# A bidirectional recurrence: the order in which TensorE and ScalarE take its keys, values and gate inputs

## The reference, cut to what matters

```
def step(carry, kv):                      # a, b, m start at 0, 0, -1e38
    mm = maximum(m + w, kt)
    e1 = exp(m + w - mm)
    e2 = exp(kt - mm)
    return ((e1 * a + e2 * vt, e1 * b + e2, mm), (a, b, m))
...
kk = kt + u
M = maximum(maximum(mf, mb), kk)
ef, eb, ec = exp(mf - M), exp(mb - M), exp(kk - M)
y = (ef * af + eb * ab + ec * vt) / (ef * bf + eb * bb + ec)
```

## Time and profile before

| | |
|---|---|
| time, median of 3 runs | 491.46 us (491.12 to 492.39) |
| profiled execution, its own time | 496.69 us |
| its span, first to last instruction | 494.8 us |
| mean granted TensorE clock | 0.81 |
| TensorE busy | 400.9 us (81%) |
| VectorE busy | 391.2 us (79%) |
| ScalarE busy | 228.1 us (46%) |
| GpSimd busy | 121.9 us (25%) |

### The profile page before, as it was taken

How to read it: one execution, slowest core, us unless ns; L and a number is a source line. 1 busy time by engine, 2 the same in 40 slices (tenths; PEclk the granted TensorE clock), 3 DMA queues, 4 the chain that set the end, 5 groups by cost and what they waited for, 6 DMA issues and landing times.

```text
span 494.8 us, 9007 instructions
## 1 busy us (share of the span) xinstructions
PE 400.9 (81%) x3570; PEld 283.6 (57%) x3570; DVE 391.2 (79%) x883; ACT 228.1 (46%) x391; POOL 121.9 (25%) x182
## 2 busy tenths in 40 slices
PE   4677857989777989999992998696799178798976
PEld 4676727769663667766761443234368036656965
DVE  3899999589887845498787679988899859777974
ACT  4477373644836668845511296010293022362261
POOL 3525344042242225233313026602202020000000
PEclk9968885596757989999986899896699578588686
DMA  8545000004014000200000000000000000000000
GB/s 279 222 121 231 2 2 1 1 1 146 1 29 191 2 1 1 95 2 1 1 0 2 1 0 0 0 1 1 1 1 1 1 1 1 1 1 2 11 24 33
DMA packets 4237, 17.53 MB, mean 35 GB/s; under 512 B 858, under 2 KB 1763, under 8 KB 3683
## 3 DMA queue, kind: packets, MB, share of 16 engines
q1 hardware_dynamic: 4194, 16.95, 9.4%
HBM read 16.16 MB, written 0.79 MB: 34 GB/s over the span
## 4 chain that ended last, share of the span: by engine, by line
PE 42%; DVE 38%; ACT 8%; issue 6%; POOL 4%; DMA 1%; SPq 0%; DVEq 0%; ACTq 0%; POOLq 0%
PE PS L1523 36%; DVE R L1102 4%; POOL rstd L522 3%; PE PS L1655 2%; DVE R L1374 2%; DVE R L1376 2%; DVE R L995 2%; PE PS L1662 2%; DVE R L1427 1%; DMA T<-tok_w 1%; DVE Q L1092 1%; DVE stats L1005 1%; DVE stats L958 1%; POOL ve L519 1%; DVE xn L1015 1%
## 5 line engine op out<-in xcount | busy, mean ns | idle before, releaser
L1523 PE MATMUL PS<-Q,R 128*128 128x32 f16 (+3 forms) x1024 | 46.1, 191 | 13.7 <-DVE R L1102 10.2
L1523 PE MATMUL PS<-m,Q 128*128 128x192 f16 (+1 forms) x576 | 52.8, 247 | 2.4 <-DVE Q L1318 2.4
L1523 PEld LDWEIGHTS PS<-Q,R 64*64 64x64 f16 (+1 forms) x1024 | 44.2, 125 | 16.9 <-DVE R L1102 10.7
L1523 PEld LDWEIGHTS PS<-m,Q 128*128 128x128 f16 (+1 forms) x576 | 46.5, 97 | 11.6 <-issue 7.8
L519 POOL TENSOR_SCALAR ve<-mv 128x1 f32<-128x1 f32 x56 | 14.5, 259 | 148.1 <-DVE mv L1006 128.9
L1523 PE MATMUL PS<-X_hi,R 128*128 128x512 f16 x144 | 42.2, 399 | 0.0
L1318 DVE TENSOR_TENSOR Q<-Q 128x512 f16<-128x512 f32 x36 | 26.1, 739 | 19.6 <-ACT Q L805 19.6
L1523 PE MATMUL PS<-R,K 128*128 128x512 f32 x66 | 35.0, 653 | 6.4 <-DVE R L1416 6.4
L1523 PE MATMUL PS<-X_hi,late_a 128*128 128x512 f16 (+1 forms) x72 | 31.4, 460 | 10.2 <-DVE X_hi L1082 5.6
L800 ACT ACTIVATE Q<-PS,col 128x512 f32<-128x512 f32 x36 | 24.8, 689 | 31.5 <-PE PS L1523 31.5
L1102 DVE TENSOR_SCALAR R<-Q,K 128x1024 f16<-128x1024 f16 x80 | 37.3, 537 | 0.3
(11 more groups left out here) (231 smaller groups left out, 934.2 us busy)
## 6 DMA issues: line engine op xcount, KB each, us to landing
R<-tok_x SPq DMA_DIRECT2D x8, 480.0 KB, 3.6
T<-tok_w SPq DMA_DIRECT2D x6, 480.0 KB, 7.7
T<-late SPq DMA_DIRECT2D x1, 2632.0 KB, 8.7
T<-moe SPq DMA_DIRECT2D x1, 2304.0 KB, 8.5
T<-moe SPq DMA_DIRECT2D x1, 1728.0 KB, 8.0
T<-full SPq DMA_DIRECT2D x1, 1152.0 KB, 4.9
R<-early SPq DMA_DIRECT2D x1, 776.0 KB, 10.3
out<-H SPq DMA_DIRECT2D x4, 192.0 KB, 1.9
```

The lines of the kernel that those rows point to most:

```text
L1523: return T_.matmul(o, w, x, start=start, stop=stop, skip_group_check=True)
```

## The change

TensorE takes k and v of block 0, k of block 1, then for each block its gaps and differences; k of block 2 comes between block 0's gaps and its other differences, v of a block just ahead of that block's gaps, and all three r behind block 2. ScalarE takes its copies and exponents in the same order, so `weights(b)` now comes before `decays(b + 1)`. `plan_fills` lists the fills in this order. VectorE's and GpSimd's order stays; only the counts of `kvr_ready` that VectorE waits for are taken from the new list `KVR_ORDER`. The arithmetic is the same.

```diff
@@ plan_fills
-    for n in "kvr":
-        f.add((n, 0), by="kvr_ready")
+    def kvr(*names):
+        for name in names:
+            f.add(name, by="kvr_ready")
+
+    kvr(("k", 0), ("v", 0))
     norm("mix1", (2, 3))
-    for block in (1, 2):
-        for n in "kvr":
-            f.add((n, block), by="kvr_ready")
+    kvr(("k", 1))
     for b in range(3):
         for i in range(2):
             f.add(("gap", b, i), by="gap_read")
+        if b == 0:
+            kvr(("k", 2))
         for i in range(3):
             f.add(("over", b, i), by="ew_ready")
+        if b < 2:
+            kvr(("v", b + 1))
+    kvr(("r", 0), ("r", 1), ("r", 2))
...
+KVR_ORDER = (("k", 0), ("v", 0), ("k", 1), ("k", 2), ("v", 1), ("v", 2), ("r", 0), ("r", 1), ("r", 2))
@@ scalar
-            kvr(0)
+            kvr(("k", 0), ("v", 0))
             x_high_affine("mix1", (2, 3))
-            kvr(1)
-            for step, b in RECURRENCE_ORDER:
-                if step == "maxima":
-                    decays(b)
-                    if b == 0:
-                        kvr(2)
-                elif step == "states":
-                    weights(b)
-                elif step == "outputs":
-                    sy_high(b)
+            kvr(("k", 1))
+            for b in range(3):
+                decays(b)
+                if b == 0:
+                    kvr(("k", 2))
+                weights(b)
+                if b < 2:
+                    kvr(("v", b + 1))
+            kvr(("r", 0), ("r", 1), ("r", 2))
+            for b in range(3):
+                sy_high(b)
@@ vector
-                dve.wait_ge(kvr_ready, 3 * b + 1)
+                dve.wait_ge(kvr_ready, KVR_ORDER.index(("k", b)) + 1)
...
-                dve.wait_ge(kvr_ready, 3 * b + 2)
+                dve.wait_ge(kvr_ready, KVR_ORDER.index(("v", b)) + 1)
...
-                dve.wait_ge(kvr_ready, 3 * b + 3)
+                dve.wait_ge(kvr_ready, KVR_ORDER.index(("r", b)) + 1)
```

More of the change, by code:

```diff
@@ L825, in _, with kvr @@
                 late_high()
[L827 to L830, removed]
+            def kvr(*names):
+                for name in names:
+                    n, block = name
+                    dst, fn, sc = {"k": (rK, ACT.Copy, 1 / WS), "v": (rV, ACT.Copy, 1 / WS),
+                                   "r": (rT, ACT.Tanh, 0.5 / WS)}[n]
                     filled(name)
@@ L1815, in _, with kvr @@
             pe.wait_ge(wlo, NM + NL + 1)
[L1817 to L1822, removed]
+            def kvr(*names):
+                for name in names:
+                    n, block = name
+                    c0 = LATE["kvr"] + C * "kvr".index(n)
                     free(name)
```

## The result

The changed kernel takes 485.85 us (median of 4 runs, 485.69 to 486.51) where the kernel before, run beside it, took 491.92: a ratio of 0.988, 95% interval 0.986 to 0.990, 6.1 us. The forecast was 486.0. In two later comparisons, on two different chips, the ratio was 0.9845 (0.981 to 0.989) and 0.9877 (0.985 to 0.990). Times of different comparisons are a few us apart for the same kernel, so the forecasts of the experiments, which start from 485.9, are best read as differences, and results as ratios to the kernel before.

A forecast was written before the change was run, and what follows sets the result against it. VectorE was taken to bound the recurrence, idle 6.51 us while the first gap waited in TensorE's queue. Starting it earlier gains 5.5 us, all else nothing: 491.46 - 5.5 = 486.0 us, 8-in-10 range 483.8 to 488.6.

The forecast's parts named there:

- The first gap: TensorE, behind k1 alone: ScalarE takes it up 5.52 us earlier, VectorE's idle time before `states(0)` falls from 6.51 to about 1.0.
- the only place: VectorE in the recurrence: only its 6.51 us of idle time before `states(0)` could give it time.
- What could be late next: Later waits in the recurrence, each followed with the 5.5 us shift: operands would still arrive in time.
- The thinnest slack: Block 1's first gap exponents ready at 290.3, VectorE through `maxima(2)` at 292.05 at the earliest: 1.7 us.
- The sums' slack at the reciprocal: Block 0's sums on TensorE done at 313.1; `outputs(0)` wants the first at 314.5, its reciprocal the second right behind.
- r products, banks, tables: r products in front of the sums hidden by VectorE's work, PSUM bank order and ScalarE's table loads unchanged: no cost.
- VectorE and GpSimd: Ten VectorE instructions stretched about 0.9 us each by GpSimd's products, before and after; those in `maxima(2)` move to `states(1)`: no gain.
- The rest of the kernel: Stages behind the recurrence move earlier as a whole; one low stretch of TensorE's clock could shift 1.7 us either way.
- a sign that the prediction had named for being wrong: Among the signs of being wrong: TensorE's clock low at places behind the recurrence where it was high before.
- smaller gain: Shorter usual idle time or one more low clock stretch on the chain: gain 3.8 to 4.0 us, 487.5; chance 0.17.
- given back later: Clock falls at three more places behind the recurrence, costing 5.1 us: 491.1, no change; chance 0.08.
- The bounds: Gain between 4.0 us, if TensorE ran at 2.4 GHz from 271.88, and 6.5 us, all of VectorE's idle time.

The follow-up runs named there:

- e3: Changed kernel with one product, k2, ahead of the first gap; 488.39 us, 0.9953 of the kernel before.
- e2: Against the changed kernel: only the r products put off, v1, k2 and v2 ahead of the first gap; 490.71 us, 1.002 of before.
- e0: The kernel before, unchanged, profiled a second time; an execution of 490.85 us.
- e7: Changed kernel with block 0's sums ahead of r1 and r2, and GpSimd's denominator products of blocks 1 and 2 held back; 483.56 us, 0.9852 of before.
- e1: Against the changed kernel: only block 0's gaps moved ahead, v1, r1, k2, v2 and r2 directly behind them, r0 not put off; 486.75 us, 0.9947 of before.
- e6: Changed kernel with block 0's two sums ahead of r1 and r2 on TensorE; 483.88 us, 0.9852 of before.
- e5: Changed kernel with GpSimd multiplying only 256 of 512 columns in its twelve recurrence products; 483.04 us.
- e9: Changed kernel with two idle clears on VectorE behind the recurrence, a 0.4 us delay; 487.57 us, 0.994 of before.
- e11: Changed kernel, unchanged, run again on the same chip as e8 and e9; 484.12 us, 0.9877 of before.
- e8: The kernel of e7 with r2 moved behind block 1's sums; 488.31 us, 0.9942 of before.
- e4: Changed kernel, unchanged, run again beside e5, e6 and e7; 482.79 us, 0.9845 of before.

## Why the prediction was right, point by point

- **The first gap.** Right in mechanism and nearly in size: from the first scan to `states(0)` 8.74 us where 281.12 - 271.86 = 9.26 was forecast, idle 0.46 and not 1.0. The difference goes with the clock's rise, 3.1 us behind k1's start and not 4.4. Against the second profile of before (14.28 us) the gain at this point is 5.54 us, against the first 6.04; the forecast had 5.52. The series of e3, e2 and e0 shows the cause by itself. That the idle time was "the only place" where VectorE could be given time was too strong: e7 took 2.85 us more out of the recurrence by moving GpSimd's products.
- **What could be late next.** Nothing was. The thinnest slack, at `states(1)`, was forecast at 1.7 us and is 288.86 - 287.64 = 1.2 (ScalarE is through L855 at 287.12 and the next one starts at 287.64); e1, with three products more in front, turned it into a wait of 2.06. The sums' slack at the reciprocal was 0.9 us and not 2.1.
- **r products, banks, tables.** They cost nothing, as forecast; e6 shows it for the r products.
- **VectorE and GpSimd.** Ten stretches before and ten after, none of the latter in `maxima(2)`, in sum 9.2 and 8.8 us. The difference, 0.3 to 0.4 us, is what the recurrence gained beyond the earlier start of `states(0)` (5.9 us, of which that is 5.5). The stretches went with GpSimd's work (e5, e7) and not with the place. The weighing went the way of the Trainium skill's "SBUF — State Buffer", section on the two sides of SBUF, by which the two engines take one port pair in turn. The prediction has it that the loser waits for the whole instruction; the stretch of 0.9 us is less than the 1.26 us that a GpSimd product takes by its own record, so that part is not shown.
- **The rest of the kernel.** Here the forecast was right by luck. It let the rest move earlier as a whole, with 1.7 us to either side for a low stretch of the clock. The rest went from 154.5 to 153.6 us, a gain of 0.9 that makes 5.9 us of recurrence into 6.8 between the profiles of e0 and changed; the timed runs differ by 6.1. It did not move as one: the clock is low at other places than before. In e0 it is low from 45.5 to 59.1 us and from 62.5 to 66.0 behind the end of the recurrence, in the changed kernel from 47.6 to 64.7. So a sign that the prediction had named for being wrong was there, and it cost nothing. With a recurrence 0.45 us longer the rest takes 2.7 us more (e9), and the kernel gains 2.9 us (0.994) and not 6: less than the 3.8 of the rival "smaller gain", whose chance was 0.17. Of "given back later" (0.08, 5.1 us given back) e2 shows the like, 1.9 us gained in the recurrence and 1.9 lost behind it. Nothing in the prediction weighed on which side of such a step the changed kernel would fall.
- **The bounds.** The lower end, 4.0 us, assumed a TensorE that is fast from k1's start. In none of the profiles taken was it. Of the 5.2 us of the first profile, of which no row showed the place, most lay ahead of the recurrence (e0).

The pieces add up to the timed ratios, though the comparisons ran on different chips. Against the changed kernel on 490 us, e3 has +1.8 and +1.7 us in its two pieces and a ratio 0.0076 higher than e11's (3.7 us); e1 +2.0 and +1.1, 0.0070 (3.4 us); e2 +3.9 and +2.8, 0.0143 (7.0 us); e8 +2.3 and +0.8, 0.0065 (3.2 us); e7 -2.9 and +2.8, and 0.0007 more than e4's (0.3 us).

## What to carry to other kernels

Where an engine takes its queue in order, write into the queue first what the engine that sets the end waits for, and count what stands in front of it: each product there cost its full length, about 1.07 us. Then ask the same of the readers' queues, since an operation put off on one engine holds up everything behind its reader on the next. And a gain in the middle of a kernel is not yet a gain at its end: compare the stages behind it, several executions each, before a variant is kept or dropped for a difference of 3 us.

## What the runs showed of the hardware that I had not expected

- The rises of TensorE's clock stand nearly fixed against this kernel's stages. In every profile but the first, the clock rose 3.1 to 3.4 us behind VectorE's first scan of the recurrence, although what lies ahead of it varied by up to 4.5 us between those profiles. The Trainium skill, "TensorE: Matmul & The Clock Gate", section "What's actually happening", has the gate free of the kernel's start. The rises came between 268.0 and 276.3 us of the span, which agrees with that. But the kernel falls into step with the clock. Why it does so was not tried. I take it to be the stages that wait for TensorE at 1.2 GHz and go on when it rises; that is argued and not shown.
- What stands behind the recurrence changes with the recurrence's length, and not monotonically: 153.6 to 153.8 us behind a recurrence of 61.3 to 61.4 us (four profiles), 156.4 behind 58.4 (two), 156.4 behind 61.9 and 65.2, 154.4 behind 60.6 and 63.6, 155.3 behind 63.2, 154.7 behind 63.4; before, 154.5 behind 67.2 and 155.3 behind 67.7. Only the first two were profiled more than once, and one delay alone was tried; there 0.45 us decided over 2.7.
- GpSimd's products with two SBUF inputs take about 0.9 us of VectorE's time each while VectorE too has two SBUF inputs, and none while it takes an operand from PSUM: the six that e7 holds back stretch neither the reciprocals nor the product of an SBUF with a PSUM operand (0.68 us). Whether PSUM matters there, or only that there is one SBUF operand, was not tried. GpSimd pays as well: its product takes 1.1 to 1.3 us beside a reciprocal and 2.2 beside scans.
